# A gated linear attention block: SP's list by due time, one store of o and one load of grown rows per pair, decay rows kept head by head

## Time and profile before

| | |
|---|---|
| median of three runs | 3543.5 us |
| profiled execution, its own time | 3546.25 us |
| its span (first to last instruction) | 3544.1 us |
| TensorE busy | 3392.6 us, 96% |
| VectorE, ScalarE, GpSimd busy | 1713.1, 1353.0, 438.9 us |
| mean granted TensorE clock | 0.981 |
| first pass, from the first to the last L560 | 85.3 to 2139.8 us |
| second pass | from 2256.7 us |

### The profile page before, as it was taken

The page is one execution under the profiler, slowest core; times in us unless marked ns, Lnnn a source line. Parts: engine busy times, 40 slices in busy tenths (PEclk is TensorE's granted clock), DMA queues, the critical chain, the costliest instruction groups (busy, mean ns, idle before and its releaser), DMA issues. The chain is left out here.

```text
span 3544.1 us, 87408 instructions
## 1 busy us (share of the span) xinstructions
PE 3392.6 (96%) x31109; PEld 3102.5 (88%) x31109; DVE 1713.1 (48%) x3988; ACT 1353.0 (38%) x3584; POOL 438.9 (12%) x723
## 2 busy tenths in 40 slices
PE   7999999999999999999999996899999999999998
PEld 6989889889888889888888885799988999899987
DVE  4333333333333333333333333667667666767676
ACT  4444434444434444434444432333332333233332
POOL 0110110110110110110100100211111121112110
PEclk9999999999999999999999997899999999999999
DMA  4332333333333333332333333521222122222220
GB/s 150 90 100 74 98 91 74 98 89 75 99 89 73 95 93 75 103 83 73 93 94 73 88 92 89 183 72 71 83 94 72 71 83 82 84 71 76 78 95 24
DMA packets 289002, 309.26 MB, mean 87 GB/s; under 512 B 34448, under 2 KB 233120, under 8 KB 284848
## 3 DMA queue, kind: packets, MB, share of 16 engines
q1 hardware_dynamic: 288944, 308.47, 30.7%
HBM read 223.40 MB, written 84.93 MB: 87 GB/s over the span
## 5 line engine op out<-in xcount | busy, mean ns | idle before, releaser
L738 DVE TENSOR_TENSOR qg<-q,grown 128x256 f32<-128x256 f32 x256 | 117.0, 457 | 750.5 <-DMA grown<-cum_dram 557.0
L655 ACT ACTIVATE prob<-cum_rows,w_cur 128x128 f32<-128x128 f32 x1024 | 327.6, 395 | 114.3 <-POOL cum_rows L830 114.0
L55 PE MATMUL psJ<-h_hi,w_g_hi 128*128 128x256 f32 x1024 | 309.8, 303 | 3.5 <-DVE h_lo L721 3.5
L55 PE MATMUL psJ<-h_hi,w_q_hi 128*128 128x256 f32 x1024 | 310.1, 303 | 0.0
L55 PE MATMUL psG<-h_hi,w_og_hi 128*128 128x256 f32 x1024 | 286.5, 280 | 7.1 <-DMA h_lo<-h_dram 7.1
L56 PE MATMUL psJ<-h_lo,w_g_hi 128*128 128x256 f32 x1024 | 290.3, 284 | 0.0
L57 PE MATMUL psJ<-h_hi,w_g_lo 128*128 128x256 f32 x1024 | 289.6, 283 | 0.0
L56 PE MATMUL psJ<-h_lo,w_q_hi 128*128 128x256 f32 x1024 | 287.2, 280 | 0.0
L57 PE MATMUL psJ<-h_hi,w_q_lo 128*128 128x256 f32 x1024 | 287.1, 280 | 0.0
L55 PE MATMUL psJ<-h_hi,w_k_hi 128*128 128x256 f32 x1024 | 286.4, 280 | 0.7 <-ACT w_new L630 0.7
L57 PE MATMUL psJ<-h_hi,w_k_lo 128*128 128x256 f32 x1024 | 286.5, 280 | 0.0
(11 more groups left out here) (215 smaller groups left out, 9457.2 us busy)
## 6 DMA issues: line engine op xcount, KB each, us to landing
cum_rows<-cum_dram SPq DMA_DIRECT2D x256, 256.0 KB, 5.6
grown<-cum_dram SPq DMA_DIRECT2D x512, 64.0 KB, 3.4
o_dram<-o SPq DMA_DIRECT2D x1024, 32.0 KB, 1.9
o_cols<-o_dram SPq DMA_DIRECT2D x32, 1024.0 KB, 5.9
an_norm_x<-in_L_attn_x_dram SPq DMA_DIRECT2D x32, 512.0 KB, 5.8
h_dram<-h_hi SPq DMA_DIRECT2D x32, 512.0 KB, 4.0
h_dram<-h_lo SPq DMA_DIRECT2D x32, 512.0 KB, 4.7
h_hi<-h_dram SPq DMA_DIRECT2D x32, 512.0 KB, 3.9
```

Of the source, the lines that this page charges most:

```text
L55: nc.tensor.matmul(out, w_hi, x_hi, start=first, stop=False)
L655: last = nc.scalar.activation(prob[:, p % 2, 2 * h + c, :], cum_rows[:, p % 4, 2 * c + h, :], ACT.Exp, bias=w_cur[:, 0, c, 2 * p + h:2 * p ...
L738: nc.vector.tensor_tensor(qg[:, p % 2, :], q[:, p, :], grown[:, p % 2, :, :].rearrange("p c t -> p (c t)"), ALU.mult).then_inc(s["qg"], 1)
```

## The change

Five things, of which the diff shows the core.

1. The columns of the decay data run head by head with the two chunks of a head beside each other (h c), where they ran chunk by chunk (c h). This concerns `g_raw`, `w_new`, `cum_dram`, `cum_rows`; `w_cur` and `w_all` keep their old order and are sorted when they are copied.
2. With that, `spread_rows` reads 2 KB in one piece for each partition, where it read two pieces of 1 KB. `grow_rows` is one DMA for both heads, with the source's dimensions [2 heads, 64 times the same, 256], where it was two of 64 partitions.
3. The store of o is one DMA of 128 partitions and 1 KB each, and no longer sorts the halves. The load of o in the second pass sorts them, by four DMAs of 64 partitions in place of one of 128.
4. In SP's list `grow_rows(p + 2)` comes right behind `spread_rows(p + 4)`. The store of pair p - 1 stands where that of pair p was, so SP waits for an `o` that is a step older. The store of `cum_out` comes behind it.
5. The semaphores' counts follow.

```diff
-        grown = sb("grown", [P, 2, NC, CH])
+        grown = sb("grown", [P, 2, T])
...
             hold(sp, s["e"], NP * i + p - 3)
-            sp.dma_start(cum_rows[:, p % 4, :, :].rearrange("p (c h) t -> p c h t", c=NC),
-                         cum_b[i, 0, :, 2 * p:2 * p + 2, :].unsqueeze(0).to_broadcast([P, NC, 2, CH])
+            sp.dma_start(cum_rows[:, p % 4, :, :].rearrange("p (h c) t -> p h (c t)", h=2),
+                         cum_b[i, 0, 2 * p:2 * p + 2, :].unsqueeze(0).to_broadcast([P, 2, T])
                          ).then_inc(spread[p % 4], 16)
 
         def grow_rows(sp, i, p):
 
             hold(sp, s["qg"], NP * i + p - 1)
-            for h in range(2):
-                sp.dma_start(grown[h * DH:(h + 1) * DH, p % 2, :, :],
-                             cum_b[i, 1, :, 2 * p + h, :].unsqueeze(0).to_broadcast([DH, NC, CH])
-                             ).then_inc(grow[p % 2], 16)
-
-        def sp_tile(sp, i, gla, proj, prep):
+            sp.dma_start(grown[:, p % 2, :],
+                         cum_b[i, 1, 2 * p:2 * p + 2, :].unsqueeze(1).to_broadcast([2, DH, T])
+                         ).then_inc(grow[p % 2], 16)
+
+        def store_o(sp, j, p):
+            sp.wait_ge(s["o"], NP * j + p + 1)
+            sp.dma_start(o_v[j, :, p, :, :], o[:, p % 2, :, :]).then_inc(store[p % 2], 16)
+
+        def sp_tile(sp, i, gla, proj, prep, opens=False):
             j = i - 1
             for p in range(NP):
                 if p == 1 and prep > 1:
@@
                 if gla and p + 4 < NP:
                     spread_rows(sp, j, p + 4)
-                if p == 6 and proj:
-                    sp.wait_ge(s["n_out"], i + 1)
-                    sp.dma_start(cum_v[i], cum_out[:, :]).then_inc(s["n_rows"], 16)
+                if gla and p + 2 < NP:
+                    grow_rows(sp, j, p + 2)
                 if p == 7 and proj:
                     sp.wait_ge(s["n_rows"], 16 * (i + 1))
                     for pair in range(4):
                         spread_rows(sp, i, pair)
                     for pair in range(2):
                         grow_rows(sp, i, pair)
-                if gla:
-                    sp.wait_ge(s["o"], NP * j + p + 1)
-                    for h in range(2):
-                        for side in range(2):
-                            sp.dma_start(o_v[j, h * DH:(h + 1) * DH, p, (h + side) % 2, :],
-                                         o[side * DH:(side + 1) * DH, p % 2, h, :]).then_inc(store[p % 2], 16)
-                    if p + 2 < NP:
-                        grow_rows(sp, j, p + 2)
+                if gla and (p > 0 or not opens):
+                    store_o(sp, j if p else j - 1, (p - 1) % NP)
+                if p == 6 and proj:
+                    sp.wait_ge(s["n_out"], i + 1)
+                    sp.dma_start(cum_v[i], cum_out[:, :]).then_inc(s["n_rows"], 16)
...
+            store_o(sp, NT - 1, NP - 1)
             for n in range(2):
-                sp.wait_ge(store[n], 64 * NP // 2 * NT)
+                sp.wait_ge(store[n], 16 * NP // 2 * NT)
...
-                                          w_new[r, 3, :].rearrange("p (c b h) -> p h c b", c=NC, h=2)[:, h, :, :])
-                nc.vector.tensor_copy(w_cur[:, :, :, :].rearrange("p a c h -> p (a c h)"),
-                                      w_new[:, 0:3, :].rearrange("p a b -> p (a b)")).then_inc(s["cur"], 1)
+                                          w_new[r, 3, :].rearrange("p (b h c) -> p h c b", c=NC, h=2)[:, h, :, :])
+                nc.vector.tensor_copy(w_cur[:, :, :, :], w_new[:, 0:3, :].rearrange("p a (h c) -> p a c h", c=NC)).then_inc(s["cur"], 1)
...
+        def load_o(sp, i):
+            for h in range(2):
+                for side in range(2):
+                    c = (h + side) % 2
+                    sp.dma_start(o[h * DH:(h + 1) * DH, :, c * CH:(c + 1) * CH],
+                                 o_v[i, side * DH:(side + 1) * DH, :, h, :]).then_inc(s["ol"], 16)
+
...
                 sp.wait_ge(s["zl"], 4 * (i + 1))
-                sp.dma_start(o[:, :, :], o_v[i + 1]).then_inc(s["ol"], 16)
+                load_o(sp, i + 1)
...
-    cum_b = cum_dram.rearrange("i (a c h) t -> i a c h t", a=2, c=NC)
+    cum_b = cum_dram.rearrange("i (a h c) t -> i a h (c t)", a=2, c=NC)
```

More of the change, by code:

```diff
@@ L437, in _ @@
             sp_tile(sp, 0, False, True, 2)
-            sp_tile(sp, 1, True, True, 2)
+            sp_tile(sp, 1, True, True, 2, True)
             with sp.Fori(2, NT - 2) as i:
@@ L640, in copy_o @@
             act.wait_ge(s["gla"], n + 1)
-            hold(act, store[p % 2], 64 * (NP // 2 * j + p // 2))
+            hold(act, store[p % 2], 16 * (NP // 2 * j + p // 2))
             nc.scalar.copy(o[:, p % 2, :, :], psO[:, :, :]).then_inc(s["o"], 1)
@@ L654, in act_tile @@
                         for h in range(2):
-                            last = nc.scalar.activation(prob[:, p % 2, 2 * h + c, :], cum_rows[:, p % 4, 2 * c + h, :], ACT.Exp,
+                            last = nc.scalar.activation(prob[:, p % 2, 2 * h + c, :], cum_rows[:, p % 4, 2 * h + c, :], ACT.Exp,
                                                         bias=w_cur[:, 0, c, 2 * p + h:2 * p + h + 1], scale=-1.0)
@@ L735, in grow_q @@
             dve.wait_ge(s["by_act"], act_done(j, ("q", p)))
-            dve.wait_ge(grow[p % 2], 32 * (NP // 2 * j + p // 2 + 1))
+            dve.wait_ge(grow[p % 2], 16 * (NP // 2 * j + p // 2 + 1))
             hold(dve, s["gla"], n - 1)
-            nc.vector.tensor_tensor(qg[:, p % 2, :], q[:, p, :], grown[:, p % 2, :, :].rearrange("p c t -> p (c t)"),
+            nc.vector.tensor_tensor(qg[:, p % 2, :], q[:, p, :], grown[:, p % 2, :],
                                     ALU.mult).then_inc(s["qg"], 1)
@@ L781, in dve_tile @@
                     dve.wait_ge(s["soft"], i + 1)
-                    nc.vector.tensor_scalar(g_raw[:, :], zt[:, 0, :, :].rearrange("p c h -> p (c h)"), -1.0, None,
+                    nc.vector.tensor_scalar(g_raw[:, :].rearrange("p (h c) -> p c h", c=NC), zt[:, 0, :, :], -1.0, None,
                                             ALU.mult).then_inc(s["g_raw"], 1)
@@ L929, in _ @@
             load_h(sp, 0)
-            sp.dma_start(o[:, :, :], o_v[0]).then_inc(s["ol"], 16)
+            load_o(sp, 0)
             sp_tile(sp, 0, True, False, True)
@@ L1033, in act_tile @@
             if att:
-                act.wait_ge(s["ol"], 16 * (i + 1))
+                act.wait_ge(s["ol"], 64 * (i + 1))
                 hold(act, s["ss"], i)
@@ L1275, in adaln_gla_block @@
             prepare(nc, t, jobs, "s")
-            output_pass(nc, t, W, x_v, o_dram, h_v, out_v)
+            output_pass(nc, t, W, x_v, o_v, h_v, out_v)
 _INS = ["L0_attn_x", "L0_attn_Wq", "L0_attn_Wk", "L0_attn_Wv", "L0_attn_Wo", "L0_attn_Wg", "L0_attn_Wog", "L0_attn_Wd",
```

## The result

The changed kernel takes 3428.2 us (median of four runs, 3427.3 to 3428.8). The kernel before took 3543.7 in the same comparison, a ratio of 0.967 (95% interval 0.9653 to 0.9686).

The account below looks back on a forecast made before the run. TensorE, busy 96%, was taken as the bound, idling mainly at L508 for `prob` behind late grown loads. 84.6 + 10.5 + 2.2 - 1.3 = 96.0 us off gave 3447.5 us by the median, range 3430 to 3490.

Parts of the forecast that it names:

- Grown loads ahead of the stores: 30 first-pass tiles: earlier loads end L508's waits for `prob` and keep the clock up; gain 84.6 us, at least 40.
- the tile without waits: Middle tile of the first pass: without L508 waits and at full clock it takes 63.62 us, against 66.44.
- its 3.8 us: Pair 3's grown load in SP's list: issued at about 1040.0 in place of 1043.78, 3.8 us earlier.
- The last tile: Last first-pass tile, no projections: five steps of 4.61 us take 23.1 in place of 33.59; gain 10.5 us.
- The end that I kept for the high clock: Last first-pass tile: steps of 3.35 us if the clock stays high; gain 16.8 us.
- The tail: End of the first pass: one store in place of several lets the next load go earlier; gain 2.2 us.
- The load of o in four parts: Second pass, first tile: smaller packets make the load slower; cost between 0 and 2.5 us, taken as 1.3.
- The range: Whole kernel: the forecast's own range is 3430 to 3470 us; reaching to half the main gain, 3430 to 3490.
- some bubbles between matmuls closing: Allowance at the range's lower end: 10 us beyond the 3440 of a high-clock last tile and free o load.
- Rivals 1 and 2: First: half the main term, 3490 us, chance 0.11. Second: VectorE's wait moves elsewhere, no change, 3543 us, chance 0.04.
- rival 3: Grown load on two DMA engines with slow packets sets the tile; slower, 3700 us at 0.14 us a packet; chance 0.05.

Follow-up runs that it names:

- The doses: Changed kernel with spare VectorE products of three sizes ahead of `prob` of pair 3 in each tile that also projects: 3463.1, 3508.0 and 3606.1 us.
- order_only: The kernel before with only SP's order changed; four stores of o, two grown loads and the old layout stay: 3431.8 us.
- late_last: The changed kernel with SP's old order in the last tile of the first pass alone: 3440.7 us.
- dose_last: The changed kernel with a spare VectorE product of 1024 columns ahead of `prob` of pairs 2 to 7 in the first pass's last tile: 3438.4 us.
- sorted_store: The changed kernel with part 3 undone: four sorting stores of o per pair, one load of o in the second pass: 3429.7 us.
- forms_only: The changed kernel with SP's old order, grown loads behind the wait for o and its one store: 3480.4 us.

## Why the prediction was wrong in size

**Grown loads ahead of the stores: right in kind, 84.6 us forecast, 99.3 measured.** Every wait went and the clock stayed up. The failing number is the tile without waits: "If L508 never waits and the clock stays up, a tile is 63.62 us". 63.62 is the busy time of a tile with two waits in it, and it holds what each wait costs beside its idle time. The tile after is 63.10. The doses show what waiting does: one wait raises the busy time from 63.10 to 63.39 us. `order_only` shows that it is not the changed forms, since its tiles without waits are 63.12 with the old ones. Two waits would make 63.7 if they add up, and the tile in the earlier trace rows, which waits 0.64 and 1.28 us, had 63.62. Over 30 tiles 0.52 us are 15.6; less the 0.9 us of idle time that stayed, that is the whole miss of 14.7 in this term.

**Which part brings it.** The prediction gave the whole term to the order. The runs say that the order alone is enough (3431.8), one store alone nearly so (3443.4), and one store with the new layout and two loads also (3434.7). They are not to be added up: each moves the load by about the 2 us that were missing, or by more. The prediction set its 3.8 us against a wait of 2.09 and did not ask whether the 2 us of part 3 alone would do. What it left out is the cover that was there already: in a middle tile of the trace after, `prob` ends at 996.28 and the next L508 starts at 998.02, 1.7 us later, and the trace before has the same 1.7 us in the steps where `grown` is in time.

**The last tile: 10.5 forecast, 16.7 measured.** Five steps take 16.92 us where they took 33.59. The mistaken step is "TensorE still idles about 1 us per step, after which the rows here show the low clock, so I take 10.5". In the earlier trace rows the clock is high behind a wait of 1.19 us and low only from the one of 5.74 us on; the step with 0.98 us of waiting was already in it. The end that I kept for the high clock, 16.8, was the right one. `late_last` and `dose_last` bear it out. From the end of these five steps to the last copy of `o` another 1.2 us went (5.6 to 4.4), which the prediction had no term for.

**The tail: 2.2 forecast, 2.7 measured.** SP's and ScalarE's timelines after, answering to the earlier trace rows:

```profile
2085.23 1.28 SPq L109 DMA_DIRECT2D s_stage<-in_L_wmod_dram  x2
```

```profile
2082.49 0.37 ACT L642 COPY o<-psP 128x256 f32<-128x256 f32 x1 [1.76 <-PE psP L493]
```

From the last copy of `o` to the next load it is 2.74 us, where it was 5.43. `sorted_store`, with the four stores, has 5.06, so it is the single store that does it.

**The load of o in four parts: 1.3 forecast, 1.9 measured,** all of it in the first tile, and not there in `sorted_store`. ScalarE waits 12.03 us where it waited 9.16, and TensorE then 1.21 us:

```profile
2141.94 2.01 ACT L1043 ACTIVATE sq<-o_cols 128x1024 f32<-128x1024 f32 x2 [12.03 <-DMA o_cols<-o_dram]
```

```profile
2145.91 0.38 PE L55 MATMUL psG<-h_hi,w_og_hi 128*128 128x256 f32 x1 [1.21 <-ACT og L1048]
```

In the later tiles the 20.6 us between issue and use covered it. The preparation is 0.9 us longer. TensorE's waits for GpSimd's `s_scaled` are 1.3 us in it in place of 0.3; why they grew stays open.

**The range.** Its lower end took the high clock in the last tile and 10 us for "some bubbles between matmuls closing", an allowance that no row gave and that was too small for the tile's 15. The two terms above are 14.7 + 6.2 = 21 us, and the small ones bring it to 22 for the span. The time came out 19.3 below the forecast, because the prediction took off 2.75 us for a profiled execution slower than the median, and that of the changed kernel stood at its median. Rivals 1 and 2 did not occur. The mechanism of rival 3 did, but not its price: the load sits on two engines. A packet of 1 KB took about 2 x 1.024 / 49 = 0.04 us per engine there, far from the 0.124 at which it would decide. The prediction let such a load land after about 7 us; the one of `forms_only` was used after 4.4.

## What to carry to other kernels

A busy engine is not at its peak around its waits: where the bound is a clean stretch, take one with no wait in it, or allow for what each wait costs beside its idle time (0.29 us here). When an engine works in order and one operand is late, ask for the operand as soon as its buffer is free; 2 us can be all that is missing, so try the smallest edit first and don't add up edits that move the same load. Look at the outer dimension of a DMA on both sides before two loads are merged into one: the merged one was slower to land here, and only its new place in the list hid it.

## What was not expected

Nearly half of the gain could have been lost in one line: the merged load costs nothing in the new order (3427.2 against 3428.2 us) and 46 us in the old one (3480.4 against 3434.7). And one wait of 1.98 us a tile brought half clock in 8 of 30 tiles, one of 0.91 us in none; 1.19 us in every step of 3.38 in the last tile did not bring it either.
